# Attention phase: the order of TensorE's work written down as strings, and value products of whole key blocks in two halves of queries

## The reference

```
q, k, v = split(layernorm(x) @ w_qkv)            # 2 batches, 16 heads, 2048 tokens, 16 per head
att = where(causal, rope(q) @ rope(k).T / 4, -inf)
o = softmax(att) @ v
```

## Time and profile before

| | |
|---|---|
| median of three runs | 1507.15 us (1505.18 to 1508.22) |
| profiled execution | 1510.13 us, its span 1508.4 us |
| granted TensorE clock, mean | 0.937 of full speed |
| attention: first reductions on DVE to the last copy on ACT | about 143 to 918 us of the span |
| last turn on DVE in attention | 875.12 us |
| PE busy, 400 to 800 us | 97% |
| DVE busy, 400 to 800 us | 96% |
| ACT busy, 400 to 800 us | 83% |

### The profile page before, as it was taken

How to read it: one execution, slowest core, us unless ns; L and a number is a source line. 1 busy time by engine, 2 the same in 40 slices (tenths; PEclk the granted TensorE clock), 3 DMA queues, 4 the chain that set the end, 5 groups by cost and what they waited for, 6 DMA issues and landing times. The chain is left out here.

```text
span 1508.4 us, 27417 instructions
## 1 busy us (share of the span) xinstructions
PE 1316.8 (87%) x9558; PEld 596.6 (40%) x9558; DVE 1272.9 (84%) x2268; ACT 998.8 (66%) x1316; POOL 324.4 (22%) x574
## 2 busy tenths in 40 slices
PE   4776999999999999999999986999767767689987
PEld 2454223232232332323322212766633334377754
DVE  6896999999999999999999933799868999665668
ACT  3452355888888888888888886666358665356642
POOL 3220000110102111020110202323100177300475
PEclk9897688999999999999999998999979889899999
DMA  6887312141423404242043024596372155686776
GB/s 206 269 257 219 57 33 45 20 81 29 83 46 41 85 7 79 46 79 49 11 76 74 12 48 116 169 315 198 136 232 86 56 171 184 215 253 205 229 227 194
DMA packets 158521, 186.16 MB, mean 123 GB/s; under 512 B 18228, under 2 KB 134708, under 8 KB 157364
## 3 DMA queue, kind: packets, MB, share of 16 engines
q1 hardware_dynamic: 135384, 151.45, 37.6%
q0 software_dynamic: 6144, 16.79, 3.6%
q10 hardware_dynamic: 16864, 16.26, 3.1%
HBM read 100.81 MB, written 83.36 MB: 122 GB/s over the span
## 5 line engine op out<-in xcount | busy, mean ns | idle before, releaser
L1334 DVE TENSOR_REDUCE att_m_part<-att_mx 128x1 f32<-128x512 f32 (+3 forms) x1152 | 680.8, 653 | 30.1 <-PE att_mx L1402 14.2
L1364 ACT ACTIVATE att_prob<-att_score,late_score_scale 128x1024 f32<-128x1024 f32 (+3 forms) x640 | 595.1, 986 | 167.2 <-PE att_score L1441 165.1
L1402 PE MATMUL att_mx<-early_kop,early_qop 48*128 48x512 f16 (+3 forms) x1280 | 354.6, 367 | 22.8 <-DVE att_m_part L1334 5.6
L1424 PE MATMUL att_pv<-att_prob,early_v 128*32 128x512 f32 (+3 forms) x2560 | 305.6, 550 | 2.0 <-POOL att_prob L1301 2.0
L1441 PE MATMUL att_score<-early_qop,early_kop 50*128 50x512 f16 (+3 forms) x1280 | 253.4, 358 | 10.3 <-ACT att_prob L1364 9.3
L1301 POOL TENSOR_SCALAR_AFFINE_SELECT att_prob<-att_prob 128x256 f32<-128x256 f32 x256 | 102.7, 406 | 671.4 <-ACT att_prob L1364 670.6
L1402 PEld LDWEIGHTS att_mx<-early_kop,early_qop 48*128 48x128 f16 x1280 | 98.5, 94 | 374.4 <-DVE att_m_part L1334 347.0
L2241 PE MATMUL rwkv_prod<-rwkv_xm,late_mixT 128*128 128x512 f32 x192 | 100.3, 675 | 37.1 <-ACT rwkv_kvr L2195 27.4
L1441 PEld LDWEIGHTS att_score<-early_qop,early_kop 50*128 50x128 f16 x1280 | 72.1, 94 | 72.5 <-ACT att_prob L1364 56.4
L1990 POOL DMA_INDIRECT rows<-rwkv_xs,routing_slot_i x64 | 69.6, 1087 | 112.2 <-DVE routing_slot_i L2082 93.0
L2462 POOL DMA_INDIRECT moe_yg<-results,routing_slot_i x64 | 64.6, 1009 | 128.6 <-issue 126.1
(11 more groups left out here) (264 smaller groups left out, 1752.9 us busy)
## 6 DMA issues: line engine op xcount, KB each, us to landing
va<-qkv_v SPq DMA_DIRECT2D x8, 1024.0 KB, 6.7
early_v<-va SPq DMA_DIRECT2D x8, 1024.0 KB, 7.5
moe_xt<-rows SPq DMA_DIRECT2D x30, 256.0 KB, 3.7
rows<-att_zeros SPq DMA_DIRECT2D x8, 928.0 KB, 6.5
early_kop<-qk SPq DMA_DIRECT2D x48, 128.0 KB, 4.4
routing_xp<-parts SPq DMA_DIRECT2D x24, 256.0 KB, 3.7
results<-moe_y ACTq DMA_DIRECT2D x24, 256.0 KB, 2.9
results<-blend_x ACTq DMA_DIRECT2D x22, 256.0 KB, 2.7
```

The source lines that it names most:

```text
L1334: nc.vector.tensor_reduce(cells[:, sides[0]:sides[-1] + 1, some], mx[:, banks[0]:banks[-1] + 1, 0:len(hps) * w].rearrange("p a (h w) -> p ...
L1364: nc.scalar.activation(prob[:, r % (PROBS * HP), :, n0:], score[:, r % 2, :, n0:], ACT.Exp, scale=late_weights.score_scale[:, 0:1])\
L1402: op = nc.tensor.matmul(bank[:, n * w:(n + 1) * w], qop[rows, slot, t, hp, i * P:(i + 1) * P], kop[rows, slot, hp, c * GT:c * GT + w], sta ...
L1424: op = nc.tensor.matmul(pv[at, n0:], v[:, slot, j, at], prob[:, (st * HP + h // 2) % (PROBS * HP), h % 2, n0:], start=(j == 0), stop=(j == ...
```

## The change

The function that planned the order is replaced by three strings of letters, `FIRST_PASSES` (502 letters), `EACH_PASS` (292, used four times) and `LAST_PASSES` (666). M, S and V stand for the next item of each kind; within a kind the order of items is as before. The value product of a step whose key block is seen by all 512 queries and isn't the first of its t (0 < j <= 4t, 24 of the 40 steps of a pass) becomes two items, one for queries 0 to 255 and one for 256 to 511. So V has 512 items instead of 320. The wait for the probabilities stays on the first half, and the signal that the step is done on the second. Counts of M (1184) and S (640) don't change.

```diff
+FIRST_PASSES = (
+    "MMMMMMMMMMMMMMMMMMMMMMMMMMMMMMMMMMMSMMSMMSMMMSMMMSSMMMVMMMVMMMVMMMMSMSMSMMSMSMMSMMMMMMMMMMMMSVMMSMSM"
+    "VMMVMSSMMVVMMMMMVMSMSMMSMMVMSMVSMSMMSMVMMVMSMSMVMSMVMVSMMSMVMSMVMMVMSMVSMMVMSSMMVMSMVMMVMMSMVMSMVMSM"
...
+EACH_PASS = (
+    "VVMSMMSMMSMVMSMMSMVMSMMSVVMSSMMMSVMMVMSMSMVMMSVVMSMMSVMMSMVVMMSMSMVMMSMVVMSSMMVMMSMVVMMSMSMMVMSMVMMS"
+    "VMSMVSMMVVMSSMMVMVMSMVMSMVMSMVMSMVMSMVMSMSMVMMSMVMMSSVMMSVSMSMVMSMVMSMSMVMMSMMSMSMVSMSMMSMSMMVVMSMSMV"
+    "MSMVMSMVMSMVMSMSMVSMMVMSMSVMMSVSMMSVMMSSMVMMSMVVMMSSMVMMSMVMMSMVMMSVMMSVMSMVMSMVSMMVMVMMSSMM")
...
+    "MSVMMSVMMSVMSMVSMMVSMMSVMSMSVMMSSMVMMVVMSSMMVMSMMVMSMSMMMSVMMSVMMSVMMSVMSMMSVMMSMVMSSMSVSVVVSVSSVVSS"
+    "SVSSVVSVVSSSVSVSSVSVSVVSVSVSSVVSSVSVVSSVVSSVVSVSVSVSVSVSVSVSVSSVVV")
...
     def matrix_order():
...
-            others = [at for at in ready if at[2] != "value"]
-            if others and min(others)[0] <= pe + soon and done["score"] // HP < done["value"] + HELD:
-                ready = others
-            when, kind = min(ready)[::2]
...
+        halves = (slice(0, GT // 2), slice(GT // 2, GT))
+        work = {"M": [("max", k) for k in range(len(entries))],
+                "S": [("score", it, st, hp) for it in range(NIT) for st in range(NS) for hp in range(HP)],
+                "V": [("value", it, st, cols) for it in range(NIT) for st, (t, j) in enumerate(steps)
+                      for cols in (halves if 0 < j <= TG * t else (slice(GT - columns(t, j), GT),))]}
+        letters = FIRST_PASSES + EACH_PASS * (NIT - 4) + LAST_PASSES
+        assert all(letters.count(kind) == len(work[kind]) for kind in work)
+        pieces = {kind: iter(work[kind]) for kind in work}
+        return [next(pieces[kind]) for kind in letters]
...
-            def products(it, st):
+            def products(it, st, cols):
...
+                if cols.start == GT - columns(t, j):
+                    if st in diagonal:
+                        pe.wait_ge(masked.sem, masked.done(it * (len(diagonal) * HP) + (diagonal.index(st) * HP + HP - 1)))
+                    else:
+                        pe.wait_ge(exp_done.sem, exp_done.done(it * NP + (st * HP + HP - 1)))
                 for h in range(HG):
                     at = slice(2 * D * h, 2 * D * (h + 1))
-                    op = nc.tensor.matmul(pv[at, n0:], v[:, slot, j, at], prob[:, (st * HP + h // 2) % (PROBS * HP), h % 2, n0:],
+                    op = nc.tensor.matmul(pv[at, cols], v[:, slot, j, at], prob[:, (st * HP + h // 2) % (PROBS * HP), h % 2, cols],
                                           start=(j == 0), stop=(j == TG * (t + 1) - 1))
-                op.then_inc(pv_done.sem, 1)
+                if cols.stop == GT:
+                    op.then_inc(pv_done.sem, 1)
```

More of the change, by code:

```diff
@@ L1042, in batch_rows @@
     return d[:, b * T:(b + 1) * T].rearrange("h (q t) -> h q t", q=P // HEADS)
+FIRST_PASSES = (
+    "MMMMMMMMMMMMMMMMMMMMMMMMMMMMMMMMMMMSMMSMMSMMMSMMMSSMMMVMMMVMMMVMMMMSMSMSMMSMSMMSMMMMMMMMMMMMSVMMSMSM"
+    "VMMVMSSMMVVMMMMMVMSMSMMSMMVMSMVSMSMMSMVMMVMSMSMVMSMVMVSMMSMVMSMVMMVMSMVSMMVMSSMMVMSMVMMVMMSMVMSMVMSM"
+    "MVSMMVSMSMMMVMSMMSMVVSMMMMMSMVMSMMMSMSMVMMVMMMMVVMMSMMSMSMSMMVMMSVMSMVMMSMVMSMMSVMMVMSMSMVMSVMMMSMMS"
+    "VMMSMVMSMVMSMVMSMVSMMVVMMSVMSMVMSMVSMMVSMMSVMMSVMSMVMMSMVMMSSMVVMMSSVMSMVMSMVSMMSMVMSMMSMSMVMSSMMMSM"
+    "VMSMVMSMSMVMSMMSVMMSVMMSVMSMVSMMVSMMSVMSMVSMSMVMSSMVMMVVMSSMMVMSMMVMSMSMMVMSMVMMSVMSMVMSMVSMMVSMMVMM"
+    "SM")
+EACH_PASS = (
+    "VVMSMMSMMSMVMSMMSMVMSMMSVVMSSMMMSVMMVMSMSMVMMSVVMSMMSVMMSMVVMMSMSMVMMSMVVMSSMMVMMSMVVMMSMSMMVMSMVMMS"
+    "VMSMVSMMVVMSSMMVMVMSMVMSMVMSMVMSMVMSMVMSMSMVMMSMVMMSSVMMSVSMSMVMSMVMSMSMVMSMMSMSMVSMSMMSMSMMVVMSMSMV"
+    "MSMVMSMVMSMVMSMSMVSMMVMSMSVMMSVSMMSVMMSSMVMMSMVVMMSSMVMMSMVMMSMVMMSVMMSVMSMVMSMVSMMVMVMMSSMM")
+LAST_PASSES = (
+    "VVMSMMSMMSMVMSMMSMVMMSMSVVMMMSSMVMMSVMSMSMVMMSVVMSMMSVMSMVMSMVMSMMSMVMSMVMSMVMMSSMVVMMMSMMVSMSMMVMMS"
+    "VMSMVSMMVVMSMVMSMVMSMVVMMSVMSMVSMMVSMMVSMMSMVMMSSMVMSMVSMSMVMSMVMVMMSSMMVSMSMMSMMVSMSMSMMMSVMVMSSMMV"
+    "MSMVMSMVSMMVSMMSVMMSVMSMVSMMSVSMMVSSMMVMSMMVVMSMSMVMSMMSMVMSMMSMVMSMVMSMVSMMVSMMSVMMVSMSMVMSMMVVMMSM"
+    "SMMVMMVMMSMVMSSMMVVSMMMVMSSMMVSMSMMVVMSMSMMVMSMSMVVMMMSVMSMMVMSMVMSMVMSMSMVVMMMSMMSVMSMMVMSMVMSMVSMM"
+    "VSMMSVMMSVMSMVMSMVSMMVVMSMVMSMVMSMVMMSSMMVMSMVSMMVSMSMVMSMVSMMSMVSMMSMMSMVMMSSMMSMVMSMVSMMSMVMMSMVMS"
+    "MSVMMSVMMSVMSMVSMMVSMMSVMSMSVMMSSMVMMVVMSSMMVMSMMVMSMSMMMSVMMSVMMSVMMSVMSMMSVMMSMVMSSMSVSVVVSVSSVVSS"
+    "SVSSVVSVVSSSVSVSSVSVSVVSVSVSSVVSSVSVVSSVVSSVVSVSVSVSVSVSVSVSVSSVVV")
 def attention_phase(nc, qk_d, va_d, att_in, feed, late_weights, parts_d, o_d, den_d, rden_d, rows_d):
@@ L1060, in attention_phase @@
     PROBS = 8
-    HELD = 3
     BANKS = 3
@@ L1167, in matrix_order @@
-        return order
+        halves = (slice(0, GT // 2), slice(GT // 2, GT))
[4 more added lines that the diff above has]
+        letters = FIRST_PASSES + EACH_PASS * (NIT - 4) + LAST_PASSES
@@ L1366, in exps @@
                     .then_inc(exp_done.sem, 1)
-            for kind, it, st, *hp in [at for at in order if at[0] != "max"]:
+            for kind, *at in order:
                 if kind == "score":
-                    exps(it, st, *hp)
-                elif st in last_step:
-                    copy_out(it, steps[st][0])
+                    exps(*at)
+                elif kind == "value" and at[1] in last_step:
+                    copy_out(at[0], steps[at[1]][0])
         @block.tensor
@@ L1410, in entry @@
                 op.then_inc(mx_done, 1)
-            def products(it, st):
+            def products(it, st, cols):
                 slot = it % 2
                 t, j = steps[st]
-                n0 = max(0, j - TG * t) * P
                 if j == 0:
                     pe.wait_ge(o_copied.sem, o_copied.freed(it * QB + t, 1))
[L1418 to L1421, removed]
+                if cols.start == GT - columns(t, j):
[3 more added lines that the diff above has]
+                        pe.wait_ge(exp_done.sem, exp_done.done(it * NP + (st * HP + HP - 1)))
                 for h in range(HG):
                     at = slice(2 * D * h, 2 * D * (h + 1))
-                    op = nc.tensor.matmul(pv[at, n0:], v[:, slot, j, at], prob[:, (st * HP + h // 2) % (PROBS * HP), h % 2, n0:],
+                    op = nc.tensor.matmul(pv[at, cols], v[:, slot, j, at], prob[:, (st * HP + h // 2) % (PROBS * HP), h % 2, cols],
                                           start=(j == 0), stop=(j == TG * (t + 1) - 1))
-                op.then_inc(pv_done.sem, 1)
+                if cols.stop == GT:
+                    op.then_inc(pv_done.sem, 1)
             def scores(it, st, hp):
```

## The result

The changed kernel takes 1469.11 us (median of 4 runs, 1466.7 to 1470.35) against 1507.68 us beside it: a ratio of 0.9739, 95% interval 0.9712 to 0.9766. It is 2.6% faster, 39 us. The side was right, the size wrong by a factor of 2.7.

What follows compares the result with a forecast made beforehand. DVE was taken to bound the attention phase. 9 us from later passes plus 5.5 us from the first gave 14.5 us off, with splitting hidden and the end 0: median 1507.15 to 1492.6 us, range 1482 to 1511.

Steps and rivals of the forecast that it cites:

- the phase gets shorter only where DVE still stands still: Attention phase: only DVE's waits, 8.5 us in the first pass and 16.6 us later, or time behind its last entry, can go.
- the time of four reductions (4 x 0.62): Even cycle of the attention phase: PE starts a value product every 2.49 us, read as four DVE reductions of 0.62 us.
- DVE never waits: Rival for the attention phase: all 25.1 us of waits go, with 1 us at the end, giving 1481 us; chance 0.13.
- I keep 45% of the 16.6 us, so 9 us go.: Passes behind the first: smaller pieces between maxima shrink DVE's waits by 9 us, bounds 0 and 16.6.
- crowding: Later passes: with PE at over 95% of its real capacity, some local crowding stays, so not all DVE waits can go.
- A split costs PE 0.15 to 0.22 us: Each value product cut in two costs PE this fixed part again, 3.6 to 5.3 us a pass.
- The total of 5.2 to 6.9 us a pass: Added PE cost of splits plus broken-up pairs of maxima (1.6 us), held to be hidden by 9.5 us of slack.
- PE becomes the bound: Rival for the passes: PE's slack is only 2.7 us, each pass grows 2.5 to 4.2 us, 1520 to 1532; chance 0.10.
- The first pass: First pass: the new order keeps PE warmer and spreads values, taking 5.5 of 8.5 us of DVE waits, bounds 0 and 8.5.
- The end: Behind the last turn: gaps hold 2.6 us, halves could win 1 us or lose as much; taken as 0.
- Three products now follow the last score: End of the phase: the possible loss from halves, as much as the 1 us they could win there.
- It fell only where PE did runs of maxima alone: PE's clock: whole from 400 to 800 us, down only in such runs; rival that it falls in the passes, chance 0.05.

Runs made afterwards that it cites:

- e1: The old kernel's planned order, each whole key block's value product cut into two halves standing side by side: 1509.0 us, ratio 0.9996.
- e3: The old kernel's planned order with halves, the second half placed behind the next maximum: 1511.6 us, ratio 1.0023.
- e7: The old planner's order with whole products up to the first score of the last pass, the changed order from there on: 1506.4 us, ratio 0.9975.
- e2: The changed kernel's strings, each value product kept whole at the place of its second half: 1514.3 us, ratio 1.0033.
- e8: The old kernel's planner, costs unchanged, placing the two halves as items of their own, without the strings: 1495.4 us, ratio 0.9923.
- e12: Old planner placing halves, four steps held, values kept from two-product diagonal maxima only while scores lead by under four steps, 300 ns limit: 1546.7 us, ratio 0.9808.
- e10: Old planner placing halves, five steps held, no value while one of the next two maxima is a two-product diagonal (600 ns limit): 1561.5 us, ratio 1.0354.
- e6: The changed order up to the first score of the second pass, the old planner's order with whole products from there on: 1501.9 us, ratio 0.9956.
- e11: The changed kernel with neighbouring halves of one key block joined into a whole product again: 1471.7 us, ratio 0.9757.

## Why the prediction was wrong

*What bounds.* Right that it is DVE, and that the phase's gain reaches the end of the kernel. The step that failed is the next one: "the phase gets shorter only where DVE still stands still", with 25.1 us of named waits as all there was. In a pass before, DVE's idle time is 91.04 - 87.43 = 3.6 us and after it 86.73 - 85.86 = 0.9. That is 2.7 of the 4.3 us. The other 1.6 us went out of the busy time, where each late bank costs 0.08 us that no idle time shows. Over 6.3 passes this hidden part is 10 us. The row for it was in the prediction: "the time of four reductions (4 x 0.62)". Three of the four starts in that very cycle came after 0.60 or 0.61 us and one after 0.68; the 0.62 was lateness that I took for DVE's own speed. I also left the waits below 0.2 us out of the sum (2.4 named of 3.6 us). So even the rival "DVE never waits", which took all 25.1 us, ended at 1481, 12 us above the result.

*"I keep 45% of the 16.6 us, so 9 us go."* The named waits fell from 16.6 to 2.0 us, so 14.6 went, and with the hidden part and the short ones the stretch from the second turn of the second pass to the last turn gave 27.65 + 1.73 = 29.4 us. This is the largest miss, 20 us. The medians miss the 14.5 us by 24, the two profiled spans by 29; 3.6 of these 29 lie outside the phase. I expected crowding because of the next point.

*The cost of splitting.* "A split costs PE 0.15 to 0.22 us": e1 shows 0 side by side, e3 0.14 where something else stands between. In the string for each pass, 5 of the 24 pairs of halves stand side by side; the other 19 cost 19 x 0.14 = 2.7 us, an estimate, in place of 3.6 to 5.3. The total of 5.2 to 6.9 us a pass was therefore too high; what the broken-up pairs of maxima cost wasn't tested alone. The other rival of that section, that PE becomes the bound, falls: PE is busy for 85.2 us of 86.7, but the only wait of DVE for it that the list names is 0.2 us. The recorded share of PE was as misleading as the text said.

*The first pass.* 5.5 us forecast, 7.5 measured, 5.4 to 7.6 over three executions with this order. The mechanism is as described: of the four value products of 1.93 us two are left, of 1.85 and 1.67; from 205 to 215 us the granted clock is 1.00 in place of 0.50; and 8.5 us of waits fell to 3.3. Not all of it: the longest wait is still 1.0 us, where I had expected less than 0.7, and from 175 to 185 us the clock is still 0.54, but with value products in the run DVE is busy throughout.

*The end.* 0 forecast, 3.0 us measured, of which the order gives 0.9 to 1.4 (e7). ACT in order of time:

```profile
843.88 3.13 ACT L1326 ACTIVATE att_prob<-att_score,late_score_scale 128x1024 f32<-128x1024 f32 x3 [0.42 <-PE att_score L1404]
846.88 0.59 ACT L1319 COPY att_o<-att_pv 128x512 f32<-128x512 f32 x1
847.35 26.89 ACT L1326 ACTIVATE att_prob<-att_score,late_score_scale 128x1024 f32<-128x1024 f32 x29
875.35 0.59 ACT L1319 COPY att_o<-att_pv 128x512 f32<-128x512 f32 x1 [1.12 <-PE att_pv L1386]
```

Between the two copies 29 exponentials run without a gap; the 1.12 before the last copy stayed. The gap of 0.72 us in the earlier trace rows was a fall of the clock: the value product ahead of that exponential takes 1.94 us there, against 1.06 at full clock.

```profile
889.13 1.94 PE L1424 MATMUL att_pv<-att_prob,early_v 128*32 128x512 f32 x8
```

"Three products now follow the last score" cost nothing that shows.

*Halves or order?* Neither alone. Whole products in the new order lose 0.3% (e2), halves side by side in the old one do nothing (e1), halves behind a fixed rule lose 0.2% (e3), a planner that may place them freely gains 0.8% (e8), the strings 2.6%. In terms of a pass, free placing takes 1.4 of the 1.6 us out of DVE's busy time, but leaves 3.4 us of idle time; the strings also take 2.5 us of that. A part of this idle time stands before the diagonal maxima of two products: 2.1 us in e8, 0.9 in e12, 0.2 in the changed kernel. What distinguishes the strings at the other places wasn't tested.

*The clock and the loads.* The clock stayed at 1.00 in the passes, as forecast. "It fell only where PE did runs of maxima alone" was a misreading: it also fell behind the last maximum, to a mean of 0.77 from 880 to 895 us, where PE does scores and values. That a late value can hold up the load of a later pass, and through it PE and its clock, wasn't among my rivals; the strings avoid it (the last value of the third pass comes behind 527 maxima, before behind 528), e10 doesn't.

## What to carry to other kernels

When one engine drains small buffers that another fills, look at the spacing of single starts in a stretch where it is surely fed, and compare it with the spacing elsewhere; idle time shown understates what can be had, since a late input can hide between records that touch. Before a difference between two traces is put down to the order, look for a stretch that ran the same order in both: here two such stretches differ by 2 us. A long operation in front of such buffers is worth cutting if the order is made anew for the pieces: the cut alone, or the order alone, can be worth nothing. If a planner may let one kind of work trail, check which transfer waits for its last item.

## What the runs showed of the hardware

- A 128x512 reduction out of PSUM lasts 0.68 us by its record, but the next one starts after 0.60 us when its input is ready, and after 0.68 when it comes just late, with no idle time shown in either case (before, 501.79 to 503.67 us).
- Value products in f32 with 32 columns of weights, four at a time: sixteen records of 256 columns take the same 1.07 us as eight of 512 (e1). The fixed 0.14 to 0.15 us is paid at the change to another kind of matmul (e3, and the kernel before).
- In e10, after a wait of PE of 2.5 us, the granted clock averaged 0.56 over 10 us and 0.67 and 0.75 over the next two tens, while DVE's busy time fell to 5.6 to 7.1 us of 10. It fell without such a wait too (0.66 from 335 to 355 us).
- The same order of work met different clocks in different executions: 0.81 to 0.84 on average over the first 105 to 108 us behind the first turn (changed, e6, e11), and the stretch was 2 us longer where it was lowest.
